# The context's layer normalisation on POOL in place of DVE, in a three-layer attention kernel on one core

## Chip, core and metric

The kernel runs on one core of a Trainium2 chip. Its time is the device time of one execution in microseconds; the median of three runs before the change is 338.59 us (337.69 to 338.70). The engines are called PE (matrix products), DVE (vector), ACT (activations), POOL (general purpose) and SP, which here only issues DMAs.

## What is computed

16 sequences of 128 tokens with 128 features go through three attention layers and an MLP. All attentions have 16 heads of 8 features.

```python
# layer 0 (cross): queries from x, keys and values from the context
xq, xkv = ada_ln(x, cond), ada_ln(ctx, cond)      # (t - mean) / sqrt(var + eps), scaled and shifted
x = x + (softmax(q(xq) @ k(xkv).T / sqrt(8)) @ v(xkv)) @ Wp + bp
# layer 1 (self): q, k and v from modulate(ln(x)); result times a gate
# layer 2 (cross): q from ln(x), k and v from ln(context)
# MLP: x + gate * (gelu(modulate(ln(x)) @ W1 + b1) @ W2 + b2)
```

The normalisation of the context, `(ctx - mean) / sqrt(var + eps)`, is made in layer 0 and again in layer 2, with another eps. The means and sums of squares of the context are kept from layer 0; in layer 2 only the root is made again.

## The kernel before

**Units and groups.** A unit is one sequence in one layer: 48 units. Four units make a group: 12 groups, 0 to 3 in layer 0, 4 to 7 in layer 1, 8 to 11 in layer 2, and four more for the MLP's input. Tokens lie on the 128 partitions. The inputs x and context lie in SBUF as `xs` and `cs`, 128 x 16 x 128 f32.

**Ticks.** Each engine runs one list of instructions, written out by a loop over ticks from -10 to 53. In tick t, unit t has its second scores and its exponentials made, unit t + 2 its first scores and row maxima, unit t + 1 its maxima turned and moved, unit t - 1 its product with the values and its division, unit t - 2 its output projection. A group's front runs ahead of its units in steps one tick apart (`front_at`): in step 0 x is normalised, in step 1 PE transposes that and DVE normalises the context (layers 0 and 2 only), in step 2 PE transposes the context's result (L348) and projects q, in step 3 k and v are projected. So every fourth tick has the same step, and group g has step 1 in tick 4g - 9.

**A normalisation.** DVE's `norm_stats` makes statistics with L735 (not for the context in layer 2) and `var_eps` (L737). POOL's `inverse_root` raises it to the power -1/2 (L902). DVE's `normalise` waits for `rstd_ready` and makes four TENSOR_SCALAR instructions (L749), one per sequence, each 128x128: subtract the mean, multiply by the root, both per-partition scalars. The last one increments `normed_ready`. PE's `transpose_normed` waits for that, takes a buffer of PSUM and makes four transposes (L348); ACT scales and shifts them (L569) or copies them (L564), which q, k (L358) and v (L366) are projected from.

**Maxima.** DVE takes the row maxima of the first scores in two halves (`row_max`, L768). POOL's `split_max` makes two bf16 parts (L909, L911). PE turns them (`turn_max`, L391), DVE copies them (`copy_max_rows`, L777), SP moves them into the stack (L281), and PE's second scores (L407) wait for that DMA.

**Order on the queues.** In a tick DVE has: `row_max` of the first half, `copy_max_rows`, `norm_stats`, `leave_rest` of k (L760), `add_branch` (L798, L801), `divide` (L783, L787), `row_max` of the second half, `normalise`, the filling of a stack (L677), gates (L807), `leave_rest` of q. POOL has: `add_gated` (L943, L945) or `add_out_bias` (L937), `inverse_root`, `split_rest` of k (L921, L923), `split_max`, `split_rest` of q, and in a few early ticks permutations (L893) and memsets (L878, L873). PE has: L407 first half, L383 first half, products with the values (L425), L391, L348, L358 for k, output projection (L447), L407 second half, the transposes of the summed output (L435), L383 second half, gates (L342), L358 for q, v, L425, L440.

**PSUM buffers.** All small PSUM results of PE take three buffers in turn, in the order `at_tick` writes out; each user waits for the reader of the buffer three uses before. So L348 can wait for DVE's reading of a gate, and L435 for `copy_max_rows`.

Of the kernel before, what the change touches and what calls it, by code (L numbers as in the profile page):

```python
# [8 lines left out]
ALU = mybir.AluOpType  # L9
# [4 lines left out]
CROSS0, SELF1, CROSS1 = range(3)  # L14
# [3 lines left out]
B, T, H = 16, 128, 128  # L18
# [6 lines left out]
PER = 4  # L25
# [28 lines left out]
def build(nc, x, ctx_1024, cond_1024, L0_xcond_Wq, L0_xcond_bq, L0_xcond_Wkv, L0_xcond_bkv,  # L54
# [12 lines left out]
    with ExitStack() as stack:  # L67
        def sb(name, shape, dt=F32):
            return stack.enter_context(nc.sbuf_tensor(name, shape, dt))

        def sem(name):
            return stack.enter_context(nc.semaphore(name))
# [8 lines left out]
        xs = sb("xs", [T, B, H])  # L81
        cs = sb("cs", [T, B, H])
# [24 lines left out]
        x_stats, c_stats = sb("x_stats", [T, PER // 2, 6]), sb("c_stats", [T, B // 2, 6])  # L107
        var_eps, rstd = sb("var_eps", [T, 2, PER]), sb("rstd", [T, 2, PER])
        normed = sb("normed", [T, 2, PER, H])
# [33 lines left out]
        setup_ps, bias_cols, mod_ready = sem("setup_ps"), sem("bias_cols"), sem("mod_ready")  # L143
        gate_ps, gate_ready = sem("gate_ps"), sem("gate_ready")
        stat_step, rstd_ready, normed_ready = sem("stat_step"), sem("rstd_ready"), sem("normed_ready")
        normed_ps, normed_t_ready = sem("normed_ps"), sem("normed_t_ready")
        qk_ps, hi_ready, rest_ready, split_ready = sem("qk_ps"), sem("hi_ready"), sem("rest_ready"), sem("split_ready")
        v_ps, v_ready = sem("v_ps"), sem("v_ready")
# [24 lines left out]
        def unit(u):  # L173
            return 0 <= u < UNITS

        def front_at(tick, step):

            g, left = divmod(tick - step + 10, PER)  # L180
            return g if left == 0 and 0 <= g < GROUPS + MLP_GROUPS and (g < GROUPS or step < 2) else None

        def layer(g):
            return g // (B // PER)

        def batches(g):
            b = PER * (g % (B // PER))
            return b, b + PER
# [5 lines left out]
        def norms_to(g, n):  # L194
            return NORMS.index((g, n)) + 1
# [28 lines left out]
        def misc(*use):  # L224

            return misc_ps[:, MISC_ORDER.index(use) % MISC, :]

        def q_in_place(eng, g):
            eng.wait_ge(q_landed[g % STACKS], 16 * MOVES * (g // STACKS + 1))
# [438 lines left out]
        def _(dve):  # L668
# [44 lines left out]
                dve.wait_ge(mod_ready, 4)  # L713
                scale_up(5)

            def norm_input(g, n):

                b0, b1 = batches(g)
                return (cs, c_stats[:, b0 // 2:b1 // 2, :]) if n else (xs, x_stats)

            def norm_stats(g, n):
                s = layer(g)
                b0, b1 = batches(g)
                src, st = norm_input(g, n)
                if s == CROSS0:
                    dve.wait_ge((x_in, c_in)[n][g], 16)

                if s in (SELF1, LAYERS) and n == 0:
                    dve.wait_ge(branch_added, B * (s - 1) + b1)
                if s == CROSS1 and n == 0:  # L730
                    dve.wait_ge(gated, 2 * b1)
                if (s, n) != (CROSS1, 1):
                    for i in range(PER // 2):
                        pair = src[:, b0 + 2 * i:b0 + 2 * i + 2, :].rearrange("t j h -> t h j")
                        stat(dve.bn_stats(st[:, i, :], pair))  # L735
                    dve.wait_ge(stat_step, stat_steps[0])
                stat(dve.tensor_scalar(var_eps[:, n, :].rearrange("t (i j) -> t i j", j=2), st[:, :, 2:6:3],  # L737
                                       1.0 / H, EPS[s], ALU.mult, ALU.add))
                assert stat_steps[0] == stat_steps_to(g, n)
# [23 lines left out]
            def row_max(u, c):  # L763
                dve.wait_ge(score_done, 2 * u + c + 1)
                if u >= 2 and c == 0:

                    dve.wait_ge(max_split, 2 * (u - 1))
                dve.tensor_reduce(neg_max[:, u % 2, :, CP * c:CP * (c + 1)],  # L768
                                  score_ps[:, :, :].rearrange("t e (a k) -> t e a k", k=T), AX.X, ALU.max,
                                  negate=True).then_inc(max_done, 1)  # L770

            def copy_max_rows(u):
                dve.wait_ge(max_ps, u + 1)
                if u >= 2:

                    max_rows_landed(dve, u - 2)
                dve.tensor_copy(max_rows[:, u % 2, :], misc("max", u)[0:2 * HEADS, 0:T // 2].bitcast(BF16)).then_inc(max_row_ready, 1)  # L777
# [45 lines left out]
            for tick in range(FIRST, LAST):  # L823
                g0, g1, g2, g3 = (front_at(tick, i) for i in range(4))
                norm = (g0, 0) if g0 is not None else (g1, 1) if (g1, 1) in NORMS else None
                if unit(tick + 2):
                    row_max(tick + 2, 0)
                if unit(tick + 1):
                    copy_max_rows(tick + 1)
                if norm:  # L830
                    norm_stats(*norm)
                if g3 is not None:
                    leave_rest(g3, 1)
                if unit(tick - 2):
                    add_branch(tick - 2)
                if unit(tick - 1):
                    divide(tick - 1)
                if unit(tick + 2):
                    row_max(tick + 2, 1)
                if tick == FIRST:  # L840
                    copy_cond()
                if tick == FIRST + 1:
                    copy_biases()
                    early_modulations()
                if norm:
                    normalise(*norm)
                if FIRST + 1 <= tick < FIRST + STACKS:
                    fill_stack(tick - FIRST)
                if tick == -2:
                    late_modulations()  # L850
                if 0 <= tick < B:
                    copy_gates(tick)
                if tick == -3:
                    dve.tensor_copy(c_rep[:, :, :], c_col[:, :].unsqueeze(2).broadcast_to([H, B, 128])).then_inc(cond_rep, 1)
                if g2 is not None:
                    leave_rest(g2, 0)
                if 0 <= tick - MLP_TICK - 2 < 4:
                    add_mlp(tick - MLP_TICK - 2)
# [3 lines left out]
        def _(pool):  # L862
# [33 lines left out]
            def inverse_root(g, n):  # L896

                pool.wait_ge(stat_step, stat_steps_to(g, n))
                if g >= 1:

                    pool.wait_ge(normed_ready, norms_to(g, n) - 1)
                pool.tensor_tensor(rstd[:, n, :], var_eps[:, n, :], minus_half[:, :], ALU.pow).then_inc(rstd_ready, 1)  # L902

            def split_max(u):

                pool.wait_ge(max_done, 2 * (u + 1))
                if u >= 2:
                    pool.wait_ge(max_ps, u - 1)
                pool.tensor_copy(max_parts[:, u % 2, :, 0, :], neg_max[:, u % 2, :, :]).then_inc(max_split, 1)  # L909
                pool.wait_ge(max_split, 2 * u + 1)  # L910
                pool.tensor_tensor(max_parts[:, u % 2, :, 1, :], neg_max[:, u % 2, :, :], max_parts[:, u % 2, :, 0, :],  # L911
                                   ALU.subtract).then_inc(max_split, 1)
# [34 lines left out]
            for tick in range(FIRST, LAST):  # L947
                g0, g1, g2, g3 = (front_at(tick, i) for i in range(4))
                norm = (g0, 0) if g0 is not None else (g1, 1) if (g1, 1) in NORMS else None
                if unit(tick - 3) and (tick - 3) // B == SELF1:  # L950
                    add_gated(tick - 3)
                if unit(tick - 2) and (tick - 2) // B != SELF1:
                    add_out_bias(tick - 2)
                if tick == FIRST:
                    permute_rows()
                if norm:
                    inverse_root(*norm)
                if tick == FIRST:
                    permute_weights(0)
                if g3 is not None:  # L960
                    split_rest(g3, 1)
                if unit(tick + 2):
                    split_max(tick + 2)
                if g2 is not None:
                    split_rest(g2, 0)
                if tick in (-4, -2):
                    permute_weights(3 + tick // 2)
                if tick in (-6, -1):
                    clear_stack(1 if tick == -6 else 2)
                if tick == -3:  # L970
                    clear_values(2)
# [30 lines left out]
```

## Time and profile before

| what | before |
|---|---|
| median of 3 runs | 338.59 us |
| profiled execution, its own time | 339.58 us |
| its span, first to last instruction | 337.8 us |
| PE busy | 282.1 us (84%) |
| DVE busy | 240.7 us (71%), 511 instructions |
| ACT busy | 204.9 us (61%) |
| POOL busy | 130.9 us (39%), 257 instructions |
| mean clock granted to PE | 0.956 of full |
| L749 for the context, 32 instructions | 11.2 us on DVE |

The profiled execution takes 1.78 us more than its span, for what lies around the first and last instruction. Busy time counts an engine's instructions, not its waiting. "Idle before" of a row is the time that its engine stood still in front of it, and the arrow names what ended that. The chain of waits is followed back from the last instruction; "issue" in it is time in which the engine waited for nothing that the profile shows. Ends of matrix products are modelled, so they may overlap by some tenths. Where a row has x4, it merges four instructions in succession.

### The profile page before, as it was taken

Reading aid. Unit: us, or ns where it says so; the run is one execution under the profiler, and the core shown is the slowest. Engines: PE = TensorE matmul, PEld = TensorE weight load, DVE = VectorE, ACT = ScalarE, POOL = GpSimd, SP = SyncE. Lnnn points to the kernel's source line nnn. Section 1 sums busy time; section 2 is a strip of 40 time slices with the busy share of each in tenths; the row PEclk is TensorE's granted clock in tenths of the full one; section 3 lists DMA queues with packets and bytes.
Section 4 is the critical chain, followed back from the end, with each engine's and each line's share of the span. In section 5 each row is a group of like instructions: output and inputs, shape, how many; then the busy total and the mean of one; then the engine's idle time right before and its main releaser. Section 6 shows DMA issues by size and latency. Waiting matters only on the chain.

```text
span 337.8 us, 10077 instructions
## 1 busy us (share of the span) xinstructions
PE 282.1 (84%) x3827; PEld 181.5 (54%) x3827; DVE 240.7 (71%) x511; ACT 204.9 (61%) x324; POOL 130.9 (39%) x257
## 2 busy tenths in 40 slices
PE   0655649989999999998989989899898888879894
PEld 0422425656666666665665666566565565534341
DVE  7754785897887878777788887978878787612103
ACT  1234126676776756768677676676677677765540
POOL 7352862525225243153653646446262131301000
PEclk9995757999999999999999999999999999999998
DMA  6943311222231322223223233132232300000013
GB/s 186 301 131 91 94 47 51 71 77 82 65 98 50 97 66 81 81 67 99 82 66 96 61 90 97 50 94 68 82 98 59 89 3 4 5 0 2 1 31 93
DMA packets 31903, 25.38 MB, mean 75 GB/s; under 512 B 4552, under 2 KB 31600, under 8 KB 31856
## 3 DMA queue, kind: packets, MB, share of 16 engines
q1 hardware_dynamic: 30240, 23.49, 24.8%
q10 hardware_dynamic: 1616, 1.25, 1.4%
q8 instruction: 31, 0.51, 0.6%
q14 instruction: 16, 0.13, 0.1%
HBM read 4.41 MB, written 1.05 MB: 16 GB/s over the span
## 4 chain that ended last, share of the span: by engine, by line
PE 42%; DVE 25%; issue 16%; POOL 5%; ACT 4%; DMA 4%; SPq 2%; ACTq 1%; DVEq 0%; POOLq 0%
DVE normed L749 8%; PE misc_ps L358 7%; PE attn_ps L425 7%; PE keyed_ps L407 4%; DMA stack_q<-max_rows 4%; DVE neg_max L768 4%; PE score_ps L472 4%; PE keyed_ps L461 4%; PE score_ps L383 3%; PE misc_ps L435 3%; PE misc_ps L366 3%; DVE x_stats L735 2%; DVE rest L760 2%; PE misc_ps L342 2%; ACT parts L583 2%
## 5 line engine op out<-in xcount | busy, mean ns | idle before, releaser
L768 DVE TENSOR_REDUCE neg_max<-score_ps 128x8 f32<-128x1024 f32 x96 | 117.4, 1223 | 14.9 <-PE score_ps L383 14.9
L603 ACT ACTIVATE probs<-keyed_ps 128x1024 f32<-128x1024 f32 x96 | 98.4, 1025 | 16.2 <-PE keyed_ps L407 14.2
L425 PE MATMUL attn_ps<-probs,values 128*32 128x128 f32 x1536 | 61.9, 279 | 0.5 <-ACT probs L603 0.5
L407 PE MATMUL keyed_ps<-stack_q,stack_k 64*128 64x128 bf16 x768 | 38.6, 220 | 13.8 <-DMA stack_q<-max_rows 13.2
L425 PEld LDWEIGHTS attn_ps<-probs,values 128*32 128x32 f32 x1536 | 36.1, 109 | 19.9 <-issue 11.2
L909 POOL CAST max_parts<-neg_max 128x16 bf16<-128x16 f32 x48 | 10.2, 213 | 89.3 <-DVE neg_max L768 89.2
L902 POOL TENSOR_TENSOR rstd<-var_eps,minus_half 128x4 f32<-128x4 f32 x24 | 24.4, 1017 | 48.7 <-DVE var_eps L737 48.7
L383 PE MATMUL score_ps<-stack_k,stack_q 62*128 62x128 bf16 x768 | 38.9, 222 | 3.7 <-DVE neg_max L768 3.7
L569 ACT ACTIVATE normed_t<-misc_ps,mod 128x128 f32<-128x128 f32 x48 | 18.1, 457 | 31.8 <-PE misc_ps L348 22.0
L407 PEld LDWEIGHTS keyed_ps<-stack_q,stack_k 64*128 64x128 bf16 x768 | 21.9, 95 | 28.1 <-DMA stack_q<-max_rows 18.3
L620 ACT ACTIVATE attn_t<-misc_ps,bcol 128x128 f32<-128x128 f32 x48 | 17.7, 368 | 28.4 <-PE misc_ps L440 26.9
L435 PE MATMUL misc_ps<-ident,summed 128*128 128x128 f32 x192 | 31.0, 284 | 2.7 <-ACT summed L611 0.3
L760 DVE SCALAR_TENSOR_TENSOR rest<-misc_ps,bcol_p,parts 128x512 f32<-128x512 f32 x24 | 17.9, 746 | 21.6 <-ACT parts L583 21.6
L348 PE MATMUL misc_ps<-ident,normed 128*128 128x128 f32 x96 | 18.3, 322 | 14.8 <-DVE normed L749 11.2
L383 PEld LDWEIGHTS score_ps<-stack_k,stack_q 62*128 62x128 bf16 x768 | 24.2, 96 | 12.1 <-issue 7.6
L358 PE MATMUL misc_ps<-normed_t,w_qk 128*128 128x512 f32 x48 | 30.7, 729 | 0.0
L611 ACT ACTIVATE summed<-attn_ps 128x512 f32<-128x512 f32 x48 | 28.4, 591 | 0.5 <-PE attn_ps L425 0.5
L923 POOL TENSOR_TENSOR parts<-rest,parts 128x512 bf16<-128x512 f32 x24 | 27.8, 1158 | 1.9
L583 ACT ACTIVATE parts<-misc_ps,bcol_p 128x512 bf16<-128x512 f32 x24 | 16.5, 687 | 18.2 <-PE misc_ps L358 18.2
L435 PEld LDWEIGHTS misc_ps<-ident,summed 128*128 128x128 f32 x192 | 20.1, 140 | 9.9 <-ACT summed L611 4.5
L921 POOL CAST parts<-rest 128x512 bf16<-128x512 f32 x24 | 14.7, 611 | 27.3 <-DVE rest L760 27.3
L749 DVE TENSOR_SCALAR normed<-xs,x_stats,rstd 128x128 f32<-128x128 f32 x64 | 21.2, 416 | 5.6 <-POOL rstd L902 5.6
(92 smaller groups left out, 393.4 us busy)
## 6 DMA issues: line engine op xcount, KB each, us to landing
stack_q<-parts SPq DMA_DIRECT2D x72, 128.0 KB, 2.4
stack_k<-parts SPq DMA_DIRECT2D x72, 128.0 KB, 2.3
stack_q<-max_rows SPq DMA_DIRECT2D x96, 4.0 KB
xs<-in_x_dram SPq DMA_DIRECT2D x4, 256.0 KB, 6.6
cs<-in_ctx_dram SPq DMA_DIRECT2D x4, 256.0 KB, 6.6
out_dram<-xs SPq DMA_DIRECT2D x4, 256.0 KB, 2.3
w<-in_L_xcond_W_mlp_dram SPq DMA_DIRECT2D x2, 256.0 KB, 4.4
wmod<-in_L_xcond_W_mod_dram ACTq DMA_DIRECT2D x1, 384.0 KB, 5.2
```

Source lines behind the costliest of these rows:

```text
L358: pe.matmul(take_misc("qk"[n], g), w_qk[:, s, n, :], normed_t[:, src, :, :], start=True, stop=True).then_inc(qk_ps, 1)
L383: mm = pe.matmul(score_ps[:, e, a * T:(a + 1) * T], stack_q[rows, g % STACKS, CP * c + a, cols], stack_k[rows, g % STACKS, CP * c + a, col ...
L407: mm = pe.matmul(keyed_ps[:, e, a * T:(a + 1) * T], stack_k[rows, g % STACKS, CP * c + a, cols], stack_q[rows, g % STACKS, CP * c + a, col ...
L425: mm = pe.matmul(attn_ps[at:at + QUAD, slot * T:(slot + 1) * T], values[:, u // PER % STACKS, u % PER, h, :], probs[:, n % 3, (CP * e + a) ...
L435: mm = pe.transpose(ps[:, i * 128:(i + 1) * 128], summed[:, u % 2, i, :], ident[:, :])
L603: act.activation(probs[:, n % 3, :], keyed_ps[:, :, :].rearrange("t e n -> t (e n)"), ACT.Exp, scale=float(D) ** -0.5).then_inc(probs_read ...
L611: act.activation(summed[:, u % 2, :, :].rearrange("p s t -> p (s t)"), attn_ps[:, :], ACT.Copy).then_inc(summed_ready, 1)
L749: ins = dve.tensor_scalar(normed[:, n, j, :], src[:, b0 + j, :], st[:, j // 2, 1 + 3 * (j % 2):2 + 3 * (j % 2)], rstd[:, n, j:j + 1], ALU. ...
L760: dve.scalar_tensor_tensor(out=rest[:, n, :], in0=misc("qk"[n], g), scalar=bcol_p[:, r:r + 1], in1=parts[:, g % 2, n, 0, :], op0=ALU.add, ...
L768: dve.tensor_reduce(neg_max[:, u % 2, :, CP * c:CP * (c + 1)], score_ps[:, :, :].rearrange("t e (a k) -> t e a k", k=T), AX.X, ALU.max, ne ...
L902: pool.tensor_tensor(rstd[:, n, :], var_eps[:, n, :], minus_half[:, :], ALU.pow).then_inc(rstd_ready, 1)
L923: pool.tensor_tensor(parts[:, g % 2, n, 2, :], rest[:, n, :], parts[:, g % 2, n, 1, :], ALU.subtract).then_inc(split_ready, 1)
```

## The change

The subtraction and the multiplication for the context go to POOL, as two TENSOR_TENSOR instructions over all four sequences of a group (128x512 f32), the mean and the root repeated along the features. A new semaphore `c_centered` lies between them. They stand on POOL's queue behind `inverse_root` and ahead of `split_rest` and `split_max`, in step 1's tick. DVE's `normalise` is called for x only. The function `norm_input` moves up so that both engines' code can call it.

```diff
--- before.py
+++ after.py
@@ -143,6 +143,7 @@
         setup_ps, bias_cols, mod_ready = sem("setup_ps"), sem("bias_cols"), sem("mod_ready")
         gate_ps, gate_ready = sem("gate_ps"), sem("gate_ready")
         stat_step, rstd_ready, normed_ready = sem("stat_step"), sem("rstd_ready"), sem("normed_ready")
+        c_centered = sem("c_centered")
         normed_ps, normed_t_ready = sem("normed_ps"), sem("normed_t_ready")
         qk_ps, hi_ready, rest_ready, split_ready = sem("qk_ps"), sem("hi_ready"), sem("rest_ready"), sem("split_ready")
         v_ps, v_ready = sem("v_ps"), sem("v_ready")
@@ -224,6 +225,11 @@
         def misc(*use):
 
             return misc_ps[:, MISC_ORDER.index(use) % MISC, :]
+
+        def norm_input(g, n):
+
+            b0, b1 = batches(g)
+            return (cs, c_stats[:, b0 // 2:b1 // 2, :]) if n else (xs, x_stats)
 
         def q_in_place(eng, g):
             eng.wait_ge(q_landed[g % STACKS], 16 * MOVES * (g // STACKS + 1))
@@ -713,11 +719,6 @@
                 dve.wait_ge(mod_ready, 4)
                 scale_up(5)
 
-            def norm_input(g, n):
-
-                b0, b1 = batches(g)
-                return (cs, c_stats[:, b0 // 2:b1 // 2, :]) if n else (xs, x_stats)
-
             def norm_stats(g, n):
                 s = layer(g)
                 b0, b1 = batches(g)
@@ -842,7 +843,7 @@
                 if tick == FIRST + 1:
                     copy_biases()
                     early_modulations()
-                if norm:
+                if norm and norm[1] == 0:
                     normalise(*norm)
                 if FIRST + 1 <= tick < FIRST + STACKS:
                     fill_stack(tick - FIRST)
@@ -901,6 +902,21 @@
                     pool.wait_ge(normed_ready, norms_to(g, n) - 1)
                 pool.tensor_tensor(rstd[:, n, :], var_eps[:, n, :], minus_half[:, :], ALU.pow).then_inc(rstd_ready, 1)
 
+            def normalise_context(g, m):
+                b0, b1 = batches(g)
+                src, st = norm_input(g, 1)
+                pool.wait_ge(rstd_ready, norms_to(g, 1))
+                if g >= 1:
+
+                    pool.wait_ge(normed_ps, norms_to(g, 1) - 1)
+                mean = st[:, :, 1:5:3].unsqueeze(3).broadcast_to([T, PER // 2, 2, H])
+                pool.tensor_tensor(normed[:, 1, :, :].rearrange("t (i j) h -> t i j h", j=2),
+                                   src[:, b0:b1, :].rearrange("t (i j) h -> t i j h", j=2), mean,
+                                   ALU.subtract).then_inc(c_centered, 1)
+                pool.wait_ge(c_centered, m + 1)
+                pool.tensor_tensor(normed[:, 1, :, :], normed[:, 1, :, :],
+                                   rstd[:, 1, :].unsqueeze(2).broadcast_to([T, PER, H]), ALU.mult).then_inc(normed_ready, 1)
+
             def split_max(u):
 
                 pool.wait_ge(max_done, 2 * (u + 1))
@@ -955,6 +971,9 @@
                     permute_rows()
                 if norm:
                     inverse_root(*norm)
+                if norm and norm[1] == 1:
+                    g = norm[0]
+                    normalise_context(g, g if layer(g) == CROSS0 else g - B // PER)
                 if tick == FIRST:
                     permute_weights(0)
                 if g3 is not None:
```

## Rows read from the trace of the kernel before

**Rows 1.** The page: PE's granted clock in tenths of full speed, in 40 slices.
```profile
PEclk9995757999999999999999999999999999999998
```

**Rows 2.** The waits, all engines: us in total, times, the longest in us.
```profile
PE keyed_ps L407 <- DMA stack_q<-max_rows: 13.2, 19, 2.1
```

**Rows 3.** The chain of waits, 170 to 192 us: start, us, what.
```profile
178.00 0.82 DVE normed L749 x3
...
180.31 0.21 DVE max_rows L777
180.52 0.14 issue
...
183.50 0.33 PE keyed_ps L407 x8
```

**Rows 4.** The timeline, 175 to 185 us: start, us, engine and operation, idle time before.
```profile
175.71 1.02 POOL L902 TENSOR_TENSOR rstd<-var_eps,minus_half 128x4 f32<-128x4 f32 x1 [0.96 <-DVE var_eps L737]
...
178.00 1.25 DVE L749 TENSOR_SCALAR normed<-cs,c_stats,rstd 128x128 f32<-128x128 f32 x4
...
178.11 0.40 PE L407 MATMUL keyed_ps<-stack_q,stack_k 64*128 64x128 bf16 x8 [0.62 <-DMA stack_q<-max_rows]
...
179.13 0.22 PE L391 MATMUL misc_ps<-ident_b,max_parts 128*32 128x128 bf16 x1
```

**Rows 5.** Groups of POOL's instructions by line and shape: us busy, mean ns of one.
```profile
L923 POOL TENSOR_TENSOR parts<-rest,parts 128x512 bf16<-128x512 f32 x24 | 27.8, 1158 | 1.9
...
L921 POOL CAST parts<-rest 128x512 bf16<-128x512 f32 x24 | 14.7, 611 | 27.3 <-DVE rest L760 27.3
L911 POOL TENSOR_TENSOR max_parts<-neg_max,max_parts 128x16 bf16<-128x16 f32 x48 | 10.5, 219 | 3.8
L909 POOL CAST max_parts<-neg_max 128x16 bf16<-128x16 f32 x48 | 10.2, 213 | 89.3 <-DVE neg_max L768 89.2
...
L945 POOL TENSOR_TENSOR xs<-xs,branch 128x128 f32<-128x128 f32 x16 | 7.3, 456 | 1.3
...
L893 POOL COPY w_qk<-wq 128x128 f32<-128x128 f32 x1 | 0.4, 391 | 0.0
```

**Rows 6.** The chain of waits, 12 to 60 us: two gaps between instructions.
```profile
20.81 0.07 issue
...
50.76 0.04 issue
```

**Rows 7.** The timeline, 10 to 35 us, group 0.
```profile
13.14 1.01 POOL L902 TENSOR_TENSOR rstd<-var_eps,minus_half 128x4 f32<-128x4 f32 x1 [1.55 <-DVE var_eps L737]
...
15.36 1.12 PE L348 MATMUL misc_ps<-ident,normed 128*128 128x128 f32 x4 [2.00 <-DVE normed L749]
...
20.91 0.75 DVE L760 SCALAR_TENSOR_TENSOR rest<-misc_ps,bcol_p,parts 128x512 f32<-128x512 f32 x1 [0.78 <-ACT parts L583]
...
21.98 0.61 POOL L921 CAST parts<-rest 128x512 bf16<-128x512 f32 x1
```

**Rows 8.** The same view, group 1.
```profile
28.15 1.01 POOL L902 TENSOR_TENSOR rstd<-var_eps,minus_half 128x4 f32<-128x4 f32 x1 [1.61 <-DVE var_eps L737]
...
30.37 1.12 PE L348 MATMUL misc_ps<-ident,normed 128*128 128x128 f32 x4 [2.00 <-DVE normed L749]
```

**Rows 9.** The timeline, 40 to 60 us, group 2.
```profile
47.00 1.01 POOL L902 TENSOR_TENSOR rstd<-var_eps,minus_half 128x4 f32<-128x4 f32 x1 [2.70 <-DVE var_eps L737]
...
48.05 2.70 DVE L749 TENSOR_SCALAR normed<-cs,c_stats,rstd 128x128 f32<-128x128 f32 x4
...
50.80 1.11 PE L348 MATMUL misc_ps<-ident,normed 128*128 128x128 f32 x4 [0.89 <-DVE normed L749]
```

**Rows 10.** The timeline, 68 to 75 us, group 3.
```profile
70.41 1.02 POOL L902 TENSOR_TENSOR rstd<-var_eps,minus_half 128x4 f32<-128x4 f32 x1 [2.63 <-DVE var_eps L737]
...
73.80 0.63 PE L348 MATMUL misc_ps<-ident,normed 128*128 128x128 f32 x4 [0.53 <-DVE gate L807]
```

**Rows 11.** Stretch, length, busy us of PE, PEld, DVE, ACT, POOL; granted clock, DMA share, GB/s.
```profile
180.00:185.00 5.00, 4.86 (x75) 2.88 (x74) 3.96 (x8) 3.73 (x7) 1.09 (x4) 1.00 0.31 88
```

## The prediction

> **What bounds the kernel now.** I read the page first: busy shares, of which PE has the largest, 84%, then the granted clock. Its digits are 9 from the eighth slice on, but lower in slices 4 to 7, where work for PE is scarce [rows 1]. Next I read the waits: PE's largest wait on a transfer is for the DMA that brings the row maxima into the stack [rows 2]. So two things alternate in the steady part: ticks that PE's own queue fills, and ticks whose length is a round trip over PE, DVE, SP and the DMA. Last I read the chain and the timeline around every normalisation of the context. There are eight, for groups 0 to 3 (first layer) and 8 to 11 (third layer). I call the tick in which one is made its c tick, and the next one, in which PE transposes the result and projects q, its q tick. In the third layer the chain runs through the c tick's normalisation and DVE's copy of the maxima to PE, and stays on PE into the next tick [rows 3]. The reader should see in rows 4 that PE idles 0.62 us only at the start of the q tick, before it meets the transpose of the maxima (L391) at 179.13.
>
> **What is removed and what is added.** DVE loses 4 instructions in each of 8 groups, 1.25 us together where nothing disturbs them [rows 4] and 2.70 in group 2 [rows 9], and the wait for the reciprocal root. POOL gets two instructions over 128x512 f32, each behind a wait. On POOL's queue they stand behind the root (L902) and in front of the split of the maxima (L909, L911). PE's L391 waits for that split, and everything of the next tick stands behind L391 on PE's queue. That is the step that costs.
>
> **Price of the two instructions.** The trace has no such instruction. Call their sum X.
> - POOL's two-input instruction over 16 elements takes 0.219 us, over 128 f32 elements 0.456 [rows 5]. That is 0.237 over 112 elements, 2.12 ns each. For 512 it makes 0.456 + 384 x 0.00212 = 1.27.
> - The one two-input instruction over 512, with a bf16 operand and a bf16 result, takes 1.158 [rows 5].
> - Below: a one-input cast over 512 takes 0.611 [rows 5]; X = 1.22. Above: as if made in four pieces of 128, 4 x 0.456 = 1.82; X = 3.65.
>
> I take 1.27 each, X = 2.54, since the operands are all f32 as in the 128-element row. L923 is just beneath it, with X = 2.32.
>
> Two gaps: POOL to POOL through a semaphore 0.07, engine to PE 0.04 [rows 6]. The split costs 0.213 + 0.07 + 0.219 = 0.50 [rows 5, 6].
>
> **Third layer, four groups.** The root ends at 175.71 + 1.02 = 176.73 [rows 4]. Then come 0.07, the subtraction, 0.07, the multiplication, 0.50 of split and 0.04: L391 can start at 177.41 + X. Before it starts at 179.13 [rows 4], so PE is late by X - 1.72. Of this 0.14 was lost anyway further on, where the PSUM buffer of the next transposes waits for DVE's copy of the maxima [rows 3]. DVE is now free earlier (its row maximum no longer waits for the normalisation) and the copy waits for L391 alone. So the loss is X - 1.86 = 0.68 a group. Nothing takes it back: PE is on the chain without a gap from there through the q tick [rows 3], and the round trip after it starts from PE's scores. From L902 to L391 it is 3.42 here [rows 4], and the timeline has the same distance in the other three groups. Sum 4X - 7.44 = 2.7.
>
> **Group 3.** The root ends at 71.43 [rows 10]. With the same 0.68 of gaps and split L391 can start at 72.11 + X, and the transposes of the context behind it (L348) 0.22 later, at 74.87 in place of 73.80: X - 1.47 = 1.07. The copy of the gates, for which L348 waited, comes earlier now.
>
> **Group 2.** The root ends at 48.01 [rows 9]; L391 at 48.69 + X, L348 another 0.26 later (PE at its lower clock): 51.49 in place of 50.80, X - 1.85 = 0.69. A gain is inside this term: DVE's four instructions took 2.70 there and held L348. POOL's clearing of the third stack moves behind both new instructions. The DMAs write that stack only when q of group 2 has been projected and split, several microseconds later, and that covers it.
>
> **Group 1.** No maxima yet. L348 can start at 28.15 + 1.01 + 0.18 + X = 29.34 + X, or 31.88 in place of 30.37 [rows 8]: X - 1.03 = 1.51. All of it is on the chain.
>
> **Group 0.** Likewise 13.14 + 1.01 + 0.18 + X = 16.87 in place of 15.36 [rows 7], 1.51. DVE's filling of the stacks, on the chain before, starts earlier and drops off. The path by ACT to the rest of k (L760) stays, and that had 0.27 to spare before POOL's cast took it: 20.91 + 0.75 + 0.05 against 21.98 [rows 7]. So X - 1.30 = 1.24.
>
> **Costed at nothing.** POOL's bias and gate additions in the q tick come about 1.2 us later; DVE's addition that reads them stands behind the copy of the maxima, which is itself later, and ends with them. If that cover were gone, it would be some tenths a group. Statistics, second-layer and MLP work, and all DMAs are untouched. DVE's saved time in the third layer brings nothing more than the 0.14: the q tick is PE's. Moving the definition of the input slices issues nothing.
>
> **Sum.** 8X - 13.09 = 7.2 us. The profiled execution took 339.58 around its span of 337.8, 0.99 over the median of 338.59. I set the sum on the median: 345.8. At X = 2.32 it is 5.5 (344.1), at X = 3.65 it is 16.1 (354.7). At X = 1.22 the third layer can give back no more than 4 x 0.14; with -0.25 (group 3), -0.63 (group 2), +0.19 (group 1) and nothing for group 0 that makes -1.25, so 337.3.
>
> **Rivals.**
> - **Idle time at the q tick's start takes it up.** PE idles 0.62 there. If the work around it shifts so that this slack serves the stall (a later L391 beside an earlier round trip), the third layer costs 4 x 0.62 less: 343.3. Against it: the stall lies after the idle time, not before. 0.14.
> - **The mean is read slowly.** The mean operand steps by three elements (12 bytes) from pair to pair and repeats within it. POOL's copies with a large stride take 0.391 for 128 [rows 5], where the casts over 16 and 512 give 0.303 by interpolation: 0.69 ns an element more. On the subtraction that is 0.35: X = 2.89, sum 10.0, 348.6. Against it: here the innermost step is 0. 0.11. The Trainium skill (GPSIMD Engine Reference, 7. Performance pitfalls for Q7 kernels) charges half as much again for reads with a step above 8 bytes; by that rule the subtraction would take an estimated 1.9, and the time would be about 350.8. The strided copy's row points the same way, with less.
> - **Four-piece price,** X = 3.65, if repeated operands break the stream: 354.7. 0.04.
> - **The clock.** With PE kept waiting the granted clock could fall from 2.4 to 1.2 GHz. In 180 to 185 it was 1.00 with PE busy 4.86 of 5 us [rows 11], and the stall leaves over 4. More likely is a late rise after group 2. One 4 us stretch of such work at the lower level costs up to 4 us: 349.8. 0.06.
> - **Faster.** POOL's pair is short and the blocked normalisation of group 2 is what counts. From X below 1.64 the sum is negative. With the cast's price it gives 337.3. For it: L749 took 2.70 in group 2, where POOL's fill of a stack ran beside it [rows 9], and DVE loses that. Against: every two-input row of POOL says more than 1.1 for 512. 0.07. The Trainium skill (SBUF — State Buffer, Who interferes with whom) has the pair of ports as an exclusive lock that one of the two holds for its whole instruction; the trace agrees (2.70 against 1.25), and by that rule the change frees DVE in group 2 alone.
>
> **Chances.** The forecast itself 0.58. What a measurement of this kernel can tell from no change is about 0.3%, 1.0 us. Faster 0.06, same 0.04, slower 0.90: all but the last rival and the mildest corner of the first end over 339.6. The range goes from 342.0 (X = 2.32 with the third layer's cost all taken up: 5.5 - 4 x 0.46 = 3.7, 342.3) to 351.0 (slow mean, or a clock that rises late); outside it are the four-piece price, the faster case and mixtures, under 0.2.
>
> **What would show it.** POOL's two instructions at 1.2 to 1.3 us each, 8 of each. In third-layer q ticks L391 waits for POOL's L911-split for 0.6 to 0.9 us, four times; the distance from the root to L391 grows from 3.42 to about 4.2. L348 waits for POOL in groups 0 and 1. DVE's busy time falls by 11 us and POOL's grows by 20. The first score maximum of the first layer and everything after it is later by 2.7 us. The second layer has its old ticks. The forecast is wrong if the two instructions fall outside 1.1 to 1.4, or if the q ticks are not longer although L391 waits.

## The result and the profile after

The changed kernel takes 341.64 us (median of 4, 341.20 to 342.56) against 338.46 for the kernel before: ratio 1.0101, 95% interval 1.0074 to 1.0129. It is slower, by 3.2 us where 7.2 were forecast, and below the range, which began at 342.0. In a second set the same kernel gave 342.27 against 339.04, ratio 1.0092 (1.0065 to 1.0119).

The page of the changed kernel, busy times and granted clock:

```profile
PE 282.1 (83%) x3827; PEld 181.0 (53%) x3827; DVE 229.9 (68%) x479; ACT 205.3 (60%) x324; POOL 146.8 (43%) x273
...
PEclk9995957999999999999999999999999999979999
```

DVE fell by 10.8 us, where 11 were forecast, and POOL rose by 15.9, where 20 were. The groups of instructions of the two new POOL lines (us busy, mean ns of one, idle time before):

```profile
L913 POOL TENSOR_TENSOR normed<-cs,c_stats 128x512 f32<-128x512 f32 x8 | 8.4, 1046 | 0.6
L917 POOL TENSOR_TENSOR normed<-normed,rstd 128x512 f32<-128x512 f32 x8 | 8.3, 1041 | 0.6
```

Together they take 1.046 + 1.041 = 2.09 us. The forecast had X = 2.54. The timeline of a c tick and the start of its q tick in the third layer, which answers to [rows 4]: first POOL, then PE and DVE (L397 is the former L391, L413 the former L407, L354 the former L348).

```profile
176.16 1.02 POOL L903 TENSOR_TENSOR rstd<-var_eps,minus_half 128x4 f32<-128x4 f32 x1 [0.96 <-DVE var_eps L738]
177.26 1.05 POOL L913 TENSOR_TENSOR normed<-cs,c_stats 128x512 f32<-128x512 f32 x1
178.39 1.04 POOL L917 TENSOR_TENSOR normed<-normed,rstd 128x512 f32<-128x512 f32 x1
179.37 0.20 POOL L925 CAST max_parts<-neg_max 128x16 bf16<-128x16 f32 x1
179.65 0.22 POOL L927 TENSOR_TENSOR max_parts<-neg_max,max_parts 128x16 bf16<-128x16 f32 x1
```

```profile
178.56 0.40 PE L413 MATMUL keyed_ps<-stack_q,stack_k 64*128 64x128 bf16 x8 [0.62 <-DMA stack_q<-max_rows]
...
179.11 0.64 PE L431 MATMUL attn_ps<-probs,values 128*32 128x128 f32 x16
179.92 0.23 PE L397 MATMUL misc_ps<-ident_b,max_parts 128*32 128x128 bf16 x1 [0.17 <-POOL max_parts L927]
180.08 0.66 PE L354 MATMUL misc_ps<-ident,normed 128*128 128x128 f32 x4
...
181.22 0.66 PE L441 MATMUL misc_ps<-ident,summed 128*128 128x128 f32 x4
```

The reader should see POOL's row without a break: root, subtraction, multiplication, both parts of the split. L397 then starts 0.05 us after the split has ended, 3.76 us after the root's start, where it was 3.42 before. PE idles 0.62 us at L413 as it did before, and the new wait of 0.17 us at L397 comes on top of that, not in its place. The chain of waits over the same stretch says the same (start, us, what):

```profile
177.26 1.05 POOL normed L913
...
178.39 1.04 POOL normed L917
...
179.57 0.04 issue
...
179.92 0.23 PE misc_ps L397
180.15 0.59 PE misc_ps L354 x4
```

In groups 0 and 1 PE waits for POOL's product (the timeline of the changed kernel, PE):

```profile
14.88 1.11 PE L354 MATMUL misc_ps<-ident,normed 128*128 128x128 f32 x4 [3.10 <-POOL normed L917]
...
30.72 1.12 PE L354 MATMUL misc_ps<-ident,normed 128*128 128x128 f32 x4 [3.09 <-POOL normed L917]
```

**Where the time came from.** The starts of the 24 root instructions (L902 before, L903 after) in the two timelines are marks on the same work, so the difference of a mark before and after shows what was lost in between. The column "after" is from the second profile of the changed kernel, whose first inputs landed as in the kernel before (the profile shown above began its work 1.6 us earlier, at 8.26 in place of 9.87, and PE's granted clock dipped to 0.57 in 300 to 304 us, which cost 0.8; neither recurred in the second profile).

```
                            root of  before  after   difference  lost by it
group 0, x                            9.87    9.68     -0.19
after context of group 0    1, x     23.78   24.24     +0.46      0.65
after context of group 1    2, x     42.07   43.52     +1.45      0.99
after context of group 2    3, x     64.96   66.55     +1.59      0.14
after context of group 3    4, x     87.51   89.66     +2.15      0.56
second layer, 4 groups      8, x    171.39  173.53     +2.14     -0.01
after context of group 8    9, x    192.17  194.45     +2.28      0.14
after group 9              10, x    212.96  215.37     +2.41      0.13
after group 10             11, x    233.74  236.28     +2.54      0.13
after group 11             MLP, 0   254.51  257.20     +2.69      0.15
last mark                  MLP, 3   306.03  308.71     +2.68
```

The sum of the losses is 2.88 us, 2.34 in the first layer and 0.55 in the third.

Not every row is equally firm. The third layer's rows are 0.13 to 0.15 us in both profiles of the changed kernel, and groups 1 and 3 agree within 0.01. Group 0 is 0.87 in the first profile. Group 2 is not resolved: the first profile has -0.36 there in place of 0.14, e_delay3, whose first layer is the changed kernel's, has +0.26, and e_third_only, whose first layer is that of the kernel before, has -0.61. What differs is when PE's clock rises: 12 to 14 us after the mark "2, x" its granted clock was 0.65 in the kernel before and 0.95 in e_third_only. A dip of the clock in the MLP, with 0.7 to 0.9 us lost, stands in three more traces, e_prices, e_full_operands and e_third_only. It is in none of the three traces in which DVE makes all normalisations; whether the change makes it more frequent is not shown.

### The profile page after: what moved, and what is told of

Its sections match the earlier page's. It is cut to its first block, busy times and chain, and to the rows that moved or that the text cites. A ratio compares the mean times of both kernels' runs of the same rounds, so it can differ in the third digit from the quotient of the medians.

```text
span 339.6 us, 10061 instructions
## 1 busy us (share of the span) xinstructions
PE 282.1 (83%) x3827; PEld 181.0 (53%) x3827; DVE 229.9 (68%) x479; ACT 205.3 (60%) x324; POOL 146.8 (43%) x273
## 4 chain that ended last, share of the span: by engine, by line
PE 45%; DVE 16%; issue 14%; POOL 12%; DMA 5%; ACT 4%; SPq 3%; POOLq 0%; DVEq 0%
PE misc_ps L364 8%; PE attn_ps L431 7%; PE keyed_ps L467 5%; PE keyed_ps L413 4%; DVE normed L750 4%; DMA stack_q<-max_rows 4%; PE score_ps L478 4%; PE score_ps L389 3%; POOL rstd L903 3%; PE misc_ps L372 3%; DVE neg_max L769 3%; PE misc_ps L354 3%; POOL normed L913 2%; DVE rest L761 2%; POOL normed L917 2%
## 5 line engine op out<-in xcount | busy, mean ns | idle before, releaser
L413 PE MATMUL keyed_ps<-stack_q,stack_k 64*128 64x128 bf16 x768 | 38.6, 220 | 13.9 <-DMA stack_q<-max_rows 13.3
L903 POOL TENSOR_TENSOR rstd<-var_eps,minus_half 128x4 f32<-128x4 f32 x24 | 24.4, 1017 | 48.4 <-DVE var_eps L738 48.4
L413 PEld LDWEIGHTS keyed_ps<-stack_q,stack_k 64*128 64x128 bf16 x768 | 21.9, 95 | 28.2 <-DMA stack_q<-max_rows 18.4
L441 PE MATMUL misc_ps<-ident,summed 128*128 128x128 f32 x192 | 31.2, 285 | 2.1 <-ACT summed L617 0.3
L354 PE MATMUL misc_ps<-ident,normed 128*128 128x128 f32 x96 | 18.3, 322 | 15.7 <-DVE normed L750 6.5
L364 PE MATMUL misc_ps<-normed_t,w_qk 128*128 128x512 f32 x48 | 29.6, 706 | 0.0
L441 PEld LDWEIGHTS misc_ps<-ident,summed 128*128 128x128 f32 x192 | 20.1, 140 | 9.0 <-ACT summed L617 4.5
```

Source lines behind the costliest of these rows:

```text
L354: mm = pe.transpose(ps[:, j * T:(j + 1) * T], normed[:, n, j, :], ident[:, :])
L364: pe.matmul(take_misc("qk"[n], g), w_qk[:, s, n, :], normed_t[:, src, :, :], start=True, stop=True).then_inc(qk_ps, 1)
L413: mm = pe.matmul(keyed_ps[:, e, a * T:(a + 1) * T], stack_k[rows, g % STACKS, CP * c + a, cols], stack_q[rows, g % STACKS, CP * c + a, col ...
L441: mm = pe.transpose(ps[:, i * 128:(i + 1) * 128], summed[:, u % 2, i, :], ident[:, :])
```

## The experiments

**The price of POOL's two-input instruction** (e_prices). Fourteen instructions behind POOL's last one, each behind a wait on the one before, of these forms (`...` stands for lines of an edit that are not shown):

```diff
+            forms = ((flat, cf, b, ALU.mult), (full, c, rep, ALU.mult), (pairs(full), pairs(c), mean, ALU.subtract),
+                     (flat[:, 0:256], cf[:, 0:256], b[:, 0:256], ALU.mult), (flat[:, 0:128], cf[:, 0:128], b[:, 0:128], ALU.mult),
+                     (flat[:, 0:16], cf[:, 0:16], b[:, 0:16], ALU.mult),
+                     (parts[:, 0, 0, 1, :], cf, b, ALU.subtract), (parts[:, 0, 0, 2, :], cf, parts[:, 1, 0, 2, :], ALU.subtract))
...
+            for f in forms + forms[:6]:
+                pool.tensor_tensor(*f).then_inc(timed, 1)
...
```

> The changed kernel with 14 two-input POOL instructions appended behind its last one, each behind a wait on the one before, into weights that are no longer read. They run beside the MLP, so the time should stay within 1 us of the changed kernel's 341.6. Theory 1 (the forecast's price was wrong because it was drawn from rows with a bf16 side): two full f32 operands over 512 take 1.05 us like the two instructions of the change, 128 take 0.456 and 16 take about 0.2 or more, and only the forms with a bf16 side are dearer. Theory 2 (a repeated operand is cheaper for POOL): two full f32 operands over 512 take 1.15 to 1.3, and the repeated root and mean take 1.04.

Its timeline, POOL, around the appended instructions:

```profile
330.51 1.27 POOL L1007 TENSOR_TENSOR wmod<-cs 128x512 f32<-128x512 f32 x1 [20.13 <-PE keyed_ps L468]
331.85 1.04 POOL L1007 TENSOR_TENSOR wmod<-cs,rstd 128x512 f32<-128x512 f32 x1
...
338.96 1.59 POOL L1007 TENSOR_TENSOR wmod<-cs 128x512 f32<-128x512 f32 x1
340.62 1.04 POOL L1007 TENSOR_TENSOR wmod<-cs,rstd 128x512 f32<-128x512 f32 x1
341.74 1.04 POOL L1007 TENSOR_TENSOR wmod<-cs,c_stats 128x512 f32<-128x512 f32 x1
```

and single small ones from a narrower stretch of the same timeline:

```profile
335.76 0.22 POOL L1007 TENSOR_TENSOR wmod<-cs 128x16 f32<-128x16 f32 x1
```

Two full f32 operands over 512 take 1.27 us, the very figure that the forecast's line through 16 and 128 gives. With the root or the mean repeated along the features it is 1.04. The second instruction of the full form took 1.59 and the first with the mean 1.37; beside each ran a DVE instruction with two SBUF operands (L822). Undisturbed, the same multiplication over the same context takes 1.27 with a full second operand and 1.04 with a repeated one. So theory 2 holds: a repeated operand costs POOL less, and no row of the kernel before had one. A bf16 result with two full f32 operands took 1.27 as well. Why L923, with one bf16 operand, takes 1.158 in the kernel stays open: its form took 1.48 here, but beside such DVE instructions. The expected time did not hold: 346.66 us in a single run, since the appended instructions waited for the MLP until 330.5 and ran past its end.

**Full operands in the kernel itself** (e_full_operands). Each instruction reads a full operand in place of the repeated one. The normalised context is left out.

```diff
-                                   src[:, b0:b1, :].rearrange("t (i j) h -> t i j h", j=2), mean,
-                                   ALU.subtract).then_inc(c_centered, 1)
+                                   src[:, b0:b1, :].rearrange("t (i j) h -> t i j h", j=2),
+                                   src[:, b0:b1, :].rearrange("t (i j) h -> t i j h", j=2), ALU.add).then_inc(c_centered, 1)
...
-                                   rstd[:, 1, :].unsqueeze(2).broadcast_to([T, PER, H]), ALU.mult).then_inc(normed_ready, 1)
+                                   src[:, b0:b1, :], ALU.mult).then_inc(normed_ready, 1)
```

> The changed kernel with a full f32 operand in place of the repeated mean and the repeated root in both POOL instructions (the context itself; the normalised context is left out, its values are others). If the repeated operand is all that made the forecast's price too high, each takes 1.27 us, X = 2.54, and every group loses 0.45 us more than in the changed kernel: 3.6 us over it, about 7 us over the kernel before, as the forecast had for its X. If the forecast's terms were wrong beside the price, the surplus is far from 3.6: under 2 if stalls are absorbed, over 5 if the longer stalls bring PE's clock down.

Ratio 1.0165 (1.0130 to 1.0199), 344.51 us, 2.2 more than the changed kernel beside it. The timeline of one c tick on POOL:

```profile
180.01 1.04 POOL L913 TENSOR_TENSOR normed<-cs 128x512 f32<-128x512 f32 x1
181.12 1.27 POOL L917 TENSOR_TENSOR normed<-normed,cs 128x512 f32<-128x512 f32 x1
```

The second instruction takes 1.27 as expected. The first, which reads the same region twice, takes 1.04 (it is also an addition in place of a subtraction, and which of the two matters was not separated). So X is 2.31 and not 2.54, and the expected surplus is 8 x 0.22 = 1.8 us in place of 3.6. Measured by the medians are 2.2; the dip in the MLP cost 0.7 in its profile and is no part of this. The roots' starts give 0.36 us a group in the third layer where the changed kernel has 0.14: 0.22 more for 0.22 more on POOL. In groups 0, 1 and 3 they give 0.21, 0.24 and 0.22 more. The slope of one is shown.

**A longer stall** (e_delay3). One more multiplication, whose result nobody reads, stands behind the two in the third layer's groups.

```diff
+                    if layer(g) == CROSS1:
+                        b0, b1 = batches(g)
+                        pool.tensor_tensor(spare[:, :, :], cs[:, b0:b1, :],
+                                           rstd[:, 1, :].unsqueeze(2).broadcast_to([T, PER, H]), ALU.mult)
```

> The changed kernel with one more POOL multiplication over 128x512 behind the two, in the third layer's four c ticks. If the stall at L391 is taken over one to one, every group loses another 1.0 us: 341.6 + 4.0 = 345.6, and L391 waits for the split about 1.2 us. If PE's 0.62 us of idle time at the start of the q tick takes part of it up, the loss is 0.4 a group: 343.2.

348.51 us, ratio 1.0299 (1.0269 to 1.0329): more than either expected. By the roots' starts the four third-layer groups lose 1.13, 1.13, 1.13 and 2.60 us. The first three are the changed kernel's 0.14 and 0.99 more, the whole of what the added instruction takes on POOL's queue. The idle time at the start of the q tick takes nothing up: that rival is out. In the fourth something else happens. Its timeline on PE and its busy time by stretches (length, then busy us of PE, PEld, DVE, ACT, POOL, then the granted clock):

```profile
246.12 0.40 PE L414 MATMUL keyed_ps<-stack_q,stack_k 64*128 64x128 bf16 x8 [0.62 <-DMA stack_q<-max_rows]
...
248.47 0.25 PE L398 MATMUL misc_ps<-ident_b,max_parts 128*32 128x128 bf16 x1 [1.15 <-POOL max_parts L928]
248.65 1.12 PE L355 MATMUL misc_ps<-ident,normed 128*128 128x128 f32 x4
...
250.67 1.11 PE L442 MATMUL misc_ps<-ident,summed 128*128 128x128 f32 x4
```

```profile
222.00:227.00 5.00, 3.23 (x65) 2.13 (x64) 3.08 (x5) 2.61 (x4) 4.68 (x8) 1.00 0.30 84
247.00:249.00 2.00, 0.85 (x15) 0.49 (x8) 1.22 (x2) 1.07 (x2) 1.75 (x4) 0.89 0.47 130
249.00:251.00 2.00, 2.00 (x16) 1.58 (x15) 0.29 (x1) 0.82 (x2) 0.00 (x0) 0.50 0.01 2
251.00:253.00 2.00, 2.00 (x14) 1.00 (x12) 1.15 (x3) 0.80 (x1) 0.00 (x0) 0.76 0.48 135
```

PE idled 0.62 us at L414 and 1.15 us at L398, and from 248.5 to about 252 its clock was granted at half: four transposes took 1.12 us where they take 0.66 at the full level. The group before it had the same two pauses and kept its clock. The drop cost 2.60 - 1.13 = 1.5 us.

**POOL in the first layer alone, and in the third alone** (e_first_only, e_third_only). DVE's side of e_first_only is below; e_third_only has CROSS0 in it, and POOL's call has the opposite condition.

```diff
-                if norm and norm[1] == 0:
+                if norm and (norm[1] == 0 or layer(norm[0]) == CROSS1):
                     normalise(*norm)
```

> POOL makes the context's normalisation in the first layer's four groups alone, DVE in the third layer. By the forecast's terms with the measured X = 2.09 the first layer costs 0.8 + 1.1 + 0.2 + 0.6 = 2.7 us: 341.2. If the loss lay in the third layer (0.7 a group, as the forecast had it with X = 2.54) it would be near 338.9.

> POOL makes it in the third layer's four groups alone, DVE in the first. By the same terms 4 x (2.09 - 1.86) = 0.9 us, or 0.6 as the trace of the changed kernel has it: 339.1 to 339.4. If the loss lay in the third layer: 341.

First layer alone: 341.56 against 339.37, ratio 1.0074 (1.0053 to 1.0096), 2.2 us, with 0.64, 1.07, 0.07 and 0.56 in the four groups by the roots' starts. Third alone: 340.04, ratio 1.0017 (0.9999 to 1.0034), which is no more than the measurement resolves; its trace has 0.13 to 0.15 us in each of the four groups. The first expectation had 2.7 us and overstates a little, but the split is clear: the loss is mostly the first layer's. The third layer, for which the forecast had 2.7 us of its 7.2, costs 0.6 by the marks.

**One-source instructions on POOL** (e_scalar for all eight groups; e_scalar_late with DVE for groups 0 and 1). These lines stand in place of the two TENSOR_TENSOR instructions:

```diff
+                for j in range(PER):
+                    ins = pool.tensor_scalar(normed[:, 1, j, :], src[:, b0 + j, :], st[:, j // 2, 1 + 3 * (j % 2):2 + 3 * (j % 2)],
+                                             rstd[:, 1, j:j + 1], ALU.subtract, ALU.mult)
+                ins.then_inc(normed_ready, 1)
```

> POOL makes the normalisation as DVE did, with four TENSOR_SCALAR over 128x128 (subtract, multiply by a scalar per partition), in place of two instructions over 512. If one takes what POOL's one-input casts give for 128 (0.30 us), the sum X is 1.2 in place of 2.09 and the kernel is at 337.3, faster than both. If a scalar per partition costs POOL as much as a second operand (0.46 each), X is 1.8 and the time about 339.8.

> Four TENSOR_SCALAR on POOL for groups 2, 3 and 8 to 11, DVE for groups 0 and 1, where it has nothing else to do. With 0.30 us each it keeps the gain of groups 2 and 3 (0.6 + 0.25) and of the third layer (4 x 0.14) and loses nothing in groups 0 and 1: 337.1. With 0.46 each: about 338.8.

Both expectations missed by far: 352.15 us, ratio 1.0412 (1.0384 to 1.0440), and 348.41, ratio 1.0278 (1.0247 to 1.0310). The timeline of e_scalar_late around group 3 and its clock in the next stretches:

```profile
71.60 3.13 POOL L912 TENSOR_SCALAR normed<-cs,c_stats,rstd 128x128 f32<-128x128 f32 x4
...
75.23 0.23 PE L396 MATMUL misc_ps<-ident_b,max_parts 128*32 128x128 bf16 x1 [1.92 <-POOL max_parts L923]
```

```profile
74.00:78.00 4.00, 2.77 (x27) 2.06 (x27) 0.72 (x4) 1.98 (x6) 1.50 (x4) 0.79 0.04 12
78.00:82.00 4.00, 4.00 (x51) 2.32 (x50) 2.58 (x6) 1.79 (x4) 0.41 (x2) 0.78 0.37 104
```

Four take 3.13 us, 0.79 each, where one of DVE's takes 0.34 for the same shape (the median of L749), and PE waits 1.92 us for the split. The group lost 2.88 us by the roots' starts. The term of the prediction, X - 1.47 with one gap less, gives 1.6; the rest goes with the clock, which stood at 0.79 and 0.78 in the eight microseconds after, where the kernel before has 1.00. In e_scalar two of the four third-layer groups lost 2.5 and 2.6 in place of 1.15, with such a drop each.

**What DVE's part was worth in group 2** (e_clear_later), on the kernel before:

```diff
-                if tick in (-6, -1):
+                if tick in (-6, 0):
                     clear_stack(1 if tick == -6 else 2)
```

> The kernel before with POOL's clearing of the third stack one tick later, so that it does not run beside DVE's normalisation of group 2. If that fill is what makes the four L749 take 2.70 us, they take 1.25 and the kernel gains up to 1.4 us: 337.1. If not, or if PE is bound there by other work, it stays at 338.5.

Ratio 0.9968 (0.9950 to 0.9985), about 1.1 us. DVE's row in the timeline of that group answers to [rows 9]:

```profile
46.81 1.15 DVE L749 TENSOR_SCALAR normed<-cs,c_stats,rstd 128x128 f32<-128x128 f32 x4
```

With the fill gone the four L749 take 1.15 in place of 2.70. The fill held DVE. The changed kernel has no DVE instructions there to be held, and that is how it got through group 2 at little cost.

**POOL's fills moved away from DVE's instructions** (e_fills_moved on the kernel before, e_fills_after on the changed one). The clearing of the second stack and of the third values goes behind the context's normalisation of group 1, that of the third stack to a later tick.

```diff
-                if tick in (-6, -1):
-                    clear_stack(1 if tick == -6 else 2)
-                if tick == -3:
-                    clear_values(2)
+                if tick == -5:
+                    pool.wait_ge(normed_ready, norms_to(1, 1))
+                    clear_stack(1)
+                    clear_values(2)
+                if tick == 0:
+                    clear_stack(2)
```

> The kernel before, DVE's normalisation kept, with POOL's fills moved away from DVE's TENSOR_SCALAR instructions: the second stack and the third values in tick -5 behind the context's normalisation of group 1, where POOL waits some 5 us, the third stack in tick 0. If the fills block DVE (and hold POOL's own root of group 2 up), x's L749 of group 1 falls from 2.37 to 1.25, L737 of group 2 from 2.31 to 0.17, L749 of the context of group 2 from 2.70 to 1.25: 1.1 + 2.0 + 1.4 = 4.5 us less, 334. If moving them only shifts the waits, it gains no more than the third stack alone did, about 1 us.

> The same moves on the changed kernel. The gain of the first two moves stays (3.1 us); the third brings nothing, since DVE has no normalisation of the context there: 341.6 - 3.1 = 338.5, that is slower than the moves without the change by 4.5 us.

e_fills_moved: 335.28 against 339.04, ratio 0.9876 (0.9845 to 0.9907), faster than both kernels by 1.2% and more. Its timeline on DVE and on POOL:

```profile
24.67 1.11 DVE L749 TENSOR_SCALAR normed<-xs,x_stats,rstd 128x128 f32<-128x128 f32 x4 [2.21 <-POOL rstd L902]
...
38.44 0.23 DVE L737 TENSOR_SCALAR var_eps<-x_stats 128x4 f32<-128x4 f32 x1
```

```profile
28.95 1.80 POOL L878 MEMSET stack_q<- 128x2048 uint32 x1 [1.21 <-DVE normed L749]
30.69 1.80 POOL L873 MEMSET values<- 128x2048 f32 x1
...
33.34 0.61 POOL L921 CAST parts<-rest 128x512 bf16<-128x512 f32 x1 [0.58 <-DVE rest L760]
```

The L749 of x in group 1 fell from 2.37 to 1.11 us, L737 of group 2 from 2.31 to 0.23, and POOL has its fills done when the next q arrives. The roots' starts give 1.27, 1.89 and 1.11 us gained at the three places, the last in the stretch of group 2 that is not resolved to better than about 0.6. e_fills_after came to 339.39, ratio 1.0015 (0.9996 to 1.0035), 4.1 us behind e_fills_moved. So once the fills no longer hold DVE, POOL's normalisation costs more than the 3.2 us that it cost with them: by the marks group 2 now loses 1.33 in place of 0.14, and the other groups lose what they lost. The compensation in group 2 is gone. The Trainium skill (SBUF — State Buffer, Who interferes with whom) has the shared ports as an exclusive lock between POOL and those DVE instructions that use both; the trace agrees with its 2.70, 2.37 and 2.31 us beside a fill, and 1.15, 1.11 and 0.23 without.

## Why the prediction was wrong, point by point

- **What fails is the step "Price of the two instructions", the term X.** It took 1.27 us each, X = 2.54, where 2.09 was measured; that alone takes 3.6 us off the sum.
  The price was taken "since the operands are all f32 as in the 128-element row". For full operands that line was right to the hundredth (1.27 in e_prices). But both new instructions repeat one operand along the features, and then POOL takes 1.046 and 1.041. The forecast thought of repetition only as something that could cost more (the rivals of the slow mean and of the four pieces), and L923's 1.158 served as the low case of the range, although a cast of 0.611 had been named as the bound beneath. With X = 2.32 at the least the range could not reach the measured time. The forecast's own sign, two instructions within 1.1 to 1.4 us, failed with it.
- **The sum and its slope held.** 8X - 13.09 with X = 2.09 gives 3.6 us; the trace has 2.9, the medians 3.2 and 3.2. At X = 2.31 (e_full_operands) it gives 5.4, the medians of that set 5.5.
- **Group by group**, with X = 2.09: group 0 0.79 against 0.65; group 1 1.06 against 0.99; group 2 0.24 against 0.14; group 3 0.62 against 0.56; third layer 0.23 against 0.14 each. All terms are a little high, though group 2's agreement is luck, since the marks do not resolve it. In the third layer the reason is visible: the forecast took 0.14 off for the wait on the copy of the maxima, and 0.23 went.
- **The chain was right.** L397 waits for POOL's split in the third layer, L354 for POOL in groups 0 and 1, all on PE's chain to the end of the q tick; the second layer kept its ticks (-0.01 over four groups). L397 comes 0.34 later after the root than before (3.76 against 3.42; X - 1.72 gives 0.37), and 0.23 of that is made good by L441, 1.30 behind it in place of 1.53 [rows 3, 4]. L397's own wait is 0.17, where 0.6 to 0.9 was forecast; it is 0.38 with X = 2.31 and 1.15 in e_delay3, so it follows from X too.
- **The absorbing idle time** (chance 0.14) is refuted by e_delay3 and e_full_operands: what is added on POOL comes out one to one.
- **The slow mean** did not happen: the mean's instruction took 1.046, the root's 1.041. The Trainium skill (GPSIMD Engine Reference, 7. Performance pitfalls for Q7 kernels) names the inner step as what has to stay within 8 bytes, and the innermost step of this operand is 0. The estimate of 1.9 us that the prediction drew from the rule did not come.
- **The clock** did not fall in the third layer of the changed kernel, as argued. Behind group 2 its rise moves by itself from one execution to the next, as said under the table. The rival is real all the same, where stalls are longer: e_delay3 and the e_scalar pair show it with 1.3 to 1.5 us each time.
- **Faster** needed X below 1.64. None of the forms tried on POOL came near it (2.09, 2.31, 3.13). What that rival said of group 2 was right: e_clear_later shows that the blocked normalisation cost the kernel before about 1.1 us.
- **Cover.** The stack's later clearing and the later bias additions cost nothing, as said: the second layer's ticks and the q ticks behind the stall have no further loss.

## What to carry to other kernels

An engine that is idle 61% of the time can still be the wrong place for work. Over half of the loss here, 1.64 of 2.88 us, came in groups 0 and 1, where PE had nothing else to do and waited for the moved work itself, which takes POOL 2.09 us and DVE about 1.2. The rest came where the work stands on POOL's queue in front of a short instruction on which the critical engine waits. Cost a moved instruction by its own form, repeated operands included; if no row has the form, let the range reach down to the next cheaper form and not only to the neighbour that looks alike. Look also for what the engines block one another with: here moving three fills gained more than the change cost.

## What the runs showed of the hardware that was not expected

- POOL's two-input instruction is cheaper when an operand is repeated: 1.04 us over 128x512 f32 against 1.27 with two different full ones, and also 1.04 in an addition whose two operands read the same region. From 16 to 512 elements the full form goes by 2.12 ns an element. The Trainium skill (GPSIMD Engine Reference, 3.1 Elementwise — side-by-side cycle accounting) names about 2.6 cycles an element for two inputs, an estimate of 1.11 us for 512 without dispatch; the full form's slope agrees with that within a few per cent, the repeated form is below it.
- POOL's TENSOR_SCALAR with two scalars per partition takes 0.79 us over 128x128 f32, 2.3 times DVE's median of 0.34. It is dearer than one two-input instruction of the same size (0.456), which makes one operation where TENSOR_SCALAR makes two.
- After a stall of 1.15 us behind 0.62 us of idle time PE's granted clock fell to the 1.2 GHz level for about 3.5 us in one group out of four with the same stall (e_delay3). Why in that one was not tried.
